# First layer of a two-layer kernel: one table instead of three, a running reference instead of the maximum, and the newest score clamped

## What is computed

```python
def step(buf, q_i):
    ki = jnp.concatenate([buf, jnp.zeros((B, 1, D), feature.dtype)], axis=1)
    scores = jnp.einsum('bwd,d->bw', q_i[:, None, :] * ki, w2_w) + w2_b[0]
    alpha = jax.nn.softmax(scores, axis=1)
    v_i = jnp.einsum('bwd,bw->bd', ki, alpha)
    new_buf = jnp.concatenate([buf[:, 1:, :], v_i[:, None, :]], axis=1)
    return (new_buf, v_i)
```

## Time and profile before

| | us |
|---|---|
| median of 3 runs | 3037.22 (3034.18 to 3037.38) |
| the profiled execution: its time | 3035.86 |
| the profiled execution: its span, first to last instruction | 3034.1 |
| busy in the span: VectorE | 2372.2 |
| busy in the span: TensorE (matmul) | 1531.9 |
| busy in the span: ScalarE | 1369.9 |
| busy in the span: GpSimd | 170.9 |

### The profile page before, as it was taken

How to read it: one execution, slowest core, us unless ns; L and a number is a source line. 1 busy time by engine, 2 the same in 40 slices (tenths; PEclk the granted TensorE clock), 3 DMA queues, 4 the chain that set the end, 5 groups by cost and what they waited for, 6 DMA issues and landing times.

```text
span 3034.1 us, 43821 instructions
## 1 busy us (share of the span) xinstructions
PE 1531.9 (50%) x8061; PEld 738.3 (24%) x8061; DVE 2372.2 (78%) x15872; ACT 1369.9 (45%) x3634; POOL 170.9 (6%) x259
## 2 busy tenths in 40 slices
PE   3001011011010010010159999999899988999796
PEld 1000000000000000000012224544245533445354
DVE  5999999999999999999678886777567765777523
ACT  1333333333333333333606666566665666556532
POOL 3000000000000000000101100100001000110000
PEclk9999999999999999999969999999999999999899
DMA  4000000000000000000340210020201101020100
GB/s 108 1 1 1 1 1 1 1 1 1 1 1 1 1 1 1 1 1 1 71 91 1 71 36 1 1 64 8 44 1 36 36 12 33 1 64 8 25 1 8
DMA packets 59766, 56.10 MB, mean 18 GB/s; under 512 B 6602, under 2 KB 43124, under 8 KB 59488
## 3 DMA queue, kind: packets, MB, share of 16 engines
q1 hardware_dynamic: 59488, 53.20, 7.4%
HBM read 29.98 MB, written 22.54 MB: 17 GB/s over the span
## 4 chain that ended last, share of the span: by engine, by line
PE 40%; ACT 3%; DVE 3%; issue 3%; DMA 1%; SPq 0%; ACTq 0%; DVEq 0%
PE p_o L1178 8%; PE bank L1232 8%; PE s L1213 7%; PE bank L1239 7%; PE s L1203 7%; ACT pt L951 2%; DVE nm_half L1026 2%; PE bank L1259 1%; ACT L951 1%; PE bank L1228 1%; PE bank L1251 0%; ACT hid L956 0%; PE bank L1275 0%; PE bank L1286 0%; DVE xa L1003 0%
## 5 line engine op out<-in xcount | busy, mean ns | idle before, releaser
L1026 DVE TENSOR_REDUCE nm_half<-s 128x1 f32<-128x512 f32 x1088 | 700.6, 685 | 250.0 <-PE s L1203 241.5
L951 ACT ACTIVATE pt<-s 128x512 f32<-128x512 f32 x1024 | 567.0, 596 | 416.2 <-PE s L1213 415.6
L197 ACT ACTIVATE ex<-row,nmax 128x65 f32<-128x65 f32 x960 | 336.0, 350 | 925.1 <-DVE nmax L299 837.7
L257 DVE SCALAR_TENSOR_TENSOR junk<-ex,tab 128x65 f32<-128x65 f32 x2850 | 620.7, 219 | 1.4 <-issue 0.2
L360 PE MATMUL p_s<-tab,bdg 128*128 128x32 f32 x120 | 31.9, 406 | 829.6 <-DVE tab L262 829.6
L1213 PE MATMUL s<-qs,ks 128*128 128x512 bf16 x1024 | 390.6, 389 | 68.0 <-ACT pt L951 56.4
L1203 PE MATMUL s<-ks,qs 128*128 128x512 bf16 x1088 | 389.1, 389 | 23.5 <-DMA qs<-zeros 20.3
L262 DVE TENSOR_TENSOR tab<-raw,rz 128x1 f32<-128x1 f32 (+1 forms) x1890 | 285.4, 151 | 3.2 <-issue 1.1
L1178 PE MATMUL p_o<-pt,va 128*9 128x512 f32 x2048 | 274.2, 608 | 0.1
L1239 PEld LDWEIGHTS bank<-w_W,hid 128*128 128x128 f32 x2048 | 257.8, 192 | 44.2 <-ACT hid L956 13.9
L291 DVE SCALAR_TENSOR_TENSOR junk<-ex,rz,row 128x65 f32<-128x65 f32 x930 | 265.3, 285 | 3.0 <-issue 2.7
(11 more groups left out here) (178 smaller groups left out, 1527.1 us busy)
## 6 DMA issues: line engine op xcount, KB each, us to landing
parts_dram<-parts SPq DMA_DIRECT2D x60, 256.0 KB, 3.6
qs<-parts_dram SPq DMA_DIRECT2D x38, 192.0 KB
ks<-parts_dram SPq DMA_DIRECT2D x38, 192.0 KB
h_dram<-f SPq DMA_DIRECT2D x20, 128.0 KB, 2.5
hq<-h_dram SPq DMA_DIRECT2D x5, 512.0 KB, 5.1
x<-in_x SPq DMA_DIRECT2D x4, 512.0 KB, 8.9
w_W<-in_W SPq DMA_DIRECT2D x1, 2048.0 KB
w_W<-in_W SPq DMA_DIRECT2D x8, 256.0 KB
```

The lines of the kernel that those rows point to most:

```text
L197: nc.scalar.activation(ex[:, r % 2, :], row[:, r % 2, 1:], ACT.Exp, bias=nmax[:, r % 2:r % 2 + 1], accum_out=z[:, r % 2:r % 2 + 1]).then_i ...
L257: nc.vector.scalar_tensor_tensor(junk[:, g, :], ex[:, k, :], 1.0, tab[:, g, r:r + ROW], ALU.mult, ALU.mult, accum_out=raw[:, g:g + 1]).the ...
L951: nc.scalar.activation(pt[:, i % 4, tokens(t)], s2[t][:, :], ACT.Exp, scale=SCALE).then_inc(s_exp, 1)
L1026: nc.vector.reduce_max(nm_half[:, t, head // 2 % 2, head % 2, q:q + 1], s1[k % 3][:, :], AX.X, negate=True).then_inc(s_max, 1)
```

## The change

The score plane and one coefficient plane become one table per chunk (`tab[:, c % 2, :]`, with a column more in front). A row holds negated scores until its step has been broadcast; then GpSimd multiplies its window by zero (`other` is 0 on the row's own partition, 1 elsewhere), and from its own step on the row collects coefficients: the column sum adds `rz` on the row's own partition (`at_own`). So one sum per step writes both the scores of later rows and the coefficients of earlier ones. That sum is a `tensor_tensor_reduce` with two pointer scalars, (ex * table) * rz summed from at_own on.

The maximum per row goes. In its place each row has a reference, the running minimum of the negated scores less 40 (`SPAN`), kept in the column ahead of the window, updated by VectorE (`least`) and broadcast along with the row; the exponential takes it as its bias. The newest score is clamped against it in the instruction that normalises it.

The 32 columns are coefficients over the 32 steps' "old parts" y (an exponential of the row's old scores, `e_old`, times the old vectors), so that a chunk needs: `masked`, `low_old`, `e_old`, its transpose (step 5), two block products on GpSimd (steps 6 and 7), y and its transpose on TensorE, a factor per row and `kf` at the end, one product for the scores of the next chunk instead of two, and one for the new vectors. Half of the next chunk's table is written at step 24. The pacing increments (`s_pace`) go.

VectorE, per chunk:

```diff
             for c in range(NC):
+                t = tab[:, c % 2, :]
                 dve.wait_ge(s_scores, c + 1)
...
+                nc.vector.stream_shuffle(row[:, 0, 3:3 + WIN], t[:, 1:1 + WIN], [0] * L).then_inc(s_first, 1)
+                nc.vector.stream_shuffle(row[:, 1, 2:2 + WIN], t[:, 1:1 + WIN], [1] * L).then_inc(s_first, 1)
+                dve.wait_ge(s_first, 2 * c + 1)
+                nc.vector.tensor_reduce(low[:, 0:1], row[:, 0, 3:3 + WIN], AX.X, ALU.min).then_inc(s_low, 1)
+                dve.wait_ge(s_first, 2 * c + 2)
+                nc.vector.tensor_reduce(low[:, 1:2], row[:, 1, 3:2 + WIN], AX.X, ALU.min).then_inc(s_low, 1)
+                dve.wait_ge(s_low, 2 * c + 1)
+                reference(c, 0, low[:, 0:1]).then_inc(s_ref0, 1)
+                dve.wait_ge(s_low, 2 * c + 2)
+                reference(c, 1, low[:, 1:2]).then_inc(s_ref0, 1)
+                dve.wait_ge(s_ref0, 2 * c + 2)
+                nc.vector.tensor_copy(ref[:, c % 2, 0:2], row[:, 0:2, 1]).then_inc(s_ref2, 1)
+
+                dve.wait_ge(s_masked, c + 1)
+                nc.vector.tensor_reduce(low_old[:, :], masked[:, :], AX.X, ALU.min).then_inc(s_low_old, 1)
+                dve.wait_ge(s_low_old, c + 1)
+                nc.vector.tensor_scalar(t[:, 0:1], low_old[:, :], 0.0, -SPAN, ALU.min, ALU.add).then_inc(s_base, 1)
```

VectorE, per step (what stands before is in the listing, L281 to L310):

```diff
+                    if last:
+
+                        dve.wait_ge(s_refs, (L - 2) * (c + 1))
+                        dve.wait_ge(s_ref2, c + 1)
+                        nc.vector.scalar_tensor_tensor(junk[:, 0, 0:L], ref[:, c % 2, :], 1.0, own[:, :], ALU.mult,
+                                                       ALU.mult, accum_out=ref_own[:, :]).then_inc(s_ref_own, 1)
                     dve.wait_ge(s_exp, n + 1)
                     nc.vector.reciprocal(rz[:, k:k + 1], z[:, k:k + 1]).then_inc(s_rz, 1)
                     if not last:
+                        if r:
+                            dve.wait_ge(s_row, (L - 2) * c + r)
+                        nc.vector.scalar_tensor_tensor(junk[:, 0, :], ex[:, k, 0:WIN], 1.0, row[:, 1 - k, 2:2 + WIN],
+                                                       ALU.mult, ALU.mult, accum_out=raw[:, k:k + 1]).then_inc(s_new, 1)
+
+                    dve.wait_ge(s_rz, n + 1)
+                    nc.vector.tensor_tensor(at_own[:, k:k + 1], own[:, r:r + 1], rz[:, k:k + 1], ALU.mult)\
+                        .then_inc(s_own_rz, 1)
                     if not last:
                         dve.wait_ge(s_new, (L - 1) * c + r + 1)
+                        if not r:
+                            dve.wait_ge(s_ref0, 2 * c + 2)
+                        nc.vector.tensor_scalar(row[:, 1 - k, 2 + WIN:3 + WIN], raw[:, k:k + 1], rz[:, k:k + 1],
+                                                row[:, 1 - k, 1:2], ALU.mult, ALU.max).then_inc(s_newest, 1)
+
+                    dve.wait_ge(s_own_rz, n + 1)
+                    dve.wait_ge(s_zeroed, (L - 1) * c + min(r, L - 2) + 1)
+                    if last:
+                        dve.wait_ge(s_col, n)
+                    nc.vector.tensor_tensor_reduce(junk[:, 1, :], ex[:, k, 0:WIN], t[:, 1 + r:1 + r + WIN],
+                                                   rz[:, k:k + 1], at_own[:, k:k + 1], ALU.mult, ALU.add,
+                                                   accum_out=t[:, 1 + WIN + r:2 + WIN + r]).then_inc(s_col, 1)
+                    dve.wait_ge(s_col, n + 1)
                     if r < L - 2:
+                        if r:
+                            dve.wait_ge(s_least, (L - 2) * c + r)
+                        else:
+                            dve.wait_ge(s_base, c + 1 + min(c, NC - 2))
+
+                        nc.vector.tensor_scalar(t[:, r + 1:r + 2], t[:, r + 1 + WIN:r + 2 + WIN], -SPAN, t[:, r:r + 1],
+                                                ALU.add, ALU.min).then_inc(s_least, 1)
+                        dve.wait_ge(s_least, (L - 2) * c + r + 1)
+                        nc.vector.stream_shuffle(row[:, k, 1:2 + WIN], t[:, r + 1:r + 2 + WIN], [r + 2] * L)\
                             .then_inc(s_row, 1)
+                    if r == 5:
+                        dve.wait_ge(s_eold, c + 1)
+                        nc.vector.transpose(e_old_t[:, :], e_old[:, :]).then_inc(s_eold_t, 1)
+                    if r == 24 and c + 1 < NC:
+                        dve.wait_ge(s_old, c + 1)
+                        relative(tab[:, 1 - c % 2, 1:1 + L], slice(0, L)).then_inc(s_table, 1)
+                dve.wait_ge(s_factor, c + 1)
+                nc.vector.tensor_scalar(kf[:, :], t[:, 1 + WIN:], factor[:, :], None, ALU.mult).then_inc(s_kf, 1)
```

GpSimd, per chunk (before: three copies and two block products):

```diff
             for c in range(NC):
+                t = tab[:, c % 2, :]
+                pool.wait_ge(s_table, 2 * c + 1)
+                nc.gpsimd.tensor_tensor(masked[:, :], t[:, 1:1 + WIN], tri[:, :], ALU.add).then_inc(s_masked, 1)
+
+                pool.wait_ge(s_first, 2 * c + 2)
+                nc.gpsimd.tensor_scalar(t[:, 1:1 + WIN], t[:, 1:1 + WIN], other01[:, :], None, ALU.mult)\
+                    .then_inc(s_zeroed, 1)
+                if c:
+                    pool.wait_ge(s_kf, c)
+                    blocks(bdk[:, :], kf[:, :]).then_inc(s_bdk, 1)
+                for r in range(L - 2):
+                    k = r % 2
+                    pool.wait_ge(s_row, (L - 2) * c + r + 1)
+
+                    nc.gpsimd.tensor_scalar(t[:, r + 2:r + 2 + WIN], t[:, r + 2:r + 2 + WIN], other[:, r + 2:r + 3],
+                                            None, ALU.mult).then_inc(s_zeroed, 1)
+                    nc.gpsimd.tensor_copy(ref[:, c % 2, r + 2:r + 3], row[:, k, 1:2]).then_inc(s_refs, 1)
+                    if r == 6:
+                        pool.wait_ge(s_eold_t, c + 1)
+                    if r in (6, 7):
+                        blocks(bde[:, r - 6, :], e_old_t[:, L * (r - 6):L * (r - 5)]).then_inc(s_bde, 1)
+                    if r == 20 and c + 1 < NC:
+                        nc.gpsimd.memset(tab[:, 1 - c % 2, 1 + WIN:], 0.0).then_inc(s_base, 1)
```

```diff
+                    nc.scalar.activation(ex[:, k, :], row[:, k, 3:], ACT.Exp, bias=row[:, k, 1:2], scale=-1.0,
+                                         accum_out=z[:, k:k + 1]).then_inc(s_exp, 1)
```

More of the change, by code:

```diff
@@ L55, in window_attention @@
         mask = sb("mask", [P, B, L])
+        later = sb("later", [P, B, L])
+        tri = sb("tri", [P, WIN])
+        own, other, other01 = sb("own", [P, L]), sb("other", [P, L]), sb("other01", [P, 1])
         wq = sb("wq", [P, D])
         bq = sb("bq", [P, 1])
[L58 to L61, removed]
+        w2, w2_neg = sb("w2", [P, 1]), sb("w2_neg", [P, 1])
+        b0, b0_neg = sb("b0", [P, 1]), sb("b0_neg", [P, 1])
         stats = sb("stats", [P, NK, 6])
@@ L81, in window_attention @@
         rz = sb("rz", [P, 2])
-        junk = sb("junk", [P, 4, ROW])
-        raw = sb("raw", [P, 3])
+        at_own = sb("at_own", [P, 2])
+        raw = sb("raw", [P, 2])
+        junk = sb("junk", [P, 2, WIN])
+        masked = sb("masked", [P, WIN])
+        low_old = sb("low_old", [P, 1])
+        e_old, e_old_t = sb("e_old", [P, WIN]), sb("e_old_t", [P, WIN])
+        bde = sb("bde", [P, 2, P])
+        yh, yt = sb("yh", [P, D]), sb("yt", [P, P])
+        bdg, bdk = sb("bdg", [P, P]), sb("bdk", [P, P])
+        ref_own, factor = sb("ref_own", [P, 1]), sb("factor", [P, 1])
+        kf = sb("kf", [P, L])
         pf = ps("pf", [P, 2, 4 * P])
@@ L166, in _ @@
[L166 to L172, removed]
-                pool.wait_ge(s_pv, c + 1)
-                for g in range(2):
-                    last = nc.gpsimd.tensor_tensor(
-                        bdc[:, g, :].rearrange("p (b j) -> p b j", b=B),
-                        tab[:, 1 + g, WIN:].unsqueeze(1).broadcast_to((P, B, L)), mask[:, :, :], ALU.mult)
@@ L180, in _ @@
+            pool.wait_ge(s_kf, NC)
+            blocks(bdk[:, :], kf[:, :]).then_inc(s_bdk, 1)
         @block.scalar
@@ L364, in _ @@
-            for g in range(2):
-                ins = nc.tensor.matmul(p_v[:, 0:D], bdc[:, g, :], v_all[:, NC + g, :], start=g == 0, stop=g == 1)
-            ins.then_inc(s_pv, 1)
+                    ins = nc.tensor.matmul(p_s[q, L * g:L * g + L], qt[:, k, q], vt[:, q], start=True, stop=True)
+                return ins
+            pe.wait_ge(s_qt, 8)
+            pe.wait_ge(s_vt0, 2)
+            against(2, vt1, 0)
+            against(2, vt2, 1).then_inc(s_scores, 1)
+            pe.wait_ge(s_vall, 2)
@@ L371, in middle @@
+            pe.wait_ge(s_yh, NC)
+            pe.wait_ge(s_bdk, NC)
+            nc.tensor.matmul(p_v[:, 0:D], bdk[:, :], yh[:, :], start=True, stop=True).then_inc(s_pv, 1)
 def middle(nc, io, xt, x1_dram, h_dram):
```

242 lines of the change are left out of this document (112 added, 130 removed).

## The result

The changed kernel takes 3252.76 us (median of 4 runs, 3251.04 to 3254.80), the kernel before 3037.30 (4 runs) beside it: ratio 1.0711, interval 1.0693 to 1.0730. The forecast was 3117, range 2975 to 3205. The kernel got slower, as forecast, but by 215 us instead of 80, outside the range.

The account below looks back on a forecast made before the run. The prediction took each step's chain of dependent operations (sum, new score, maximum, exponential) as the bound. Steps of 1.44 instead of 1.36 us, 900 times, gave 72, chunks 8: +80 on 3037.2, so 3117 us, range 2975 to 3205.

Parts of the forecast that it names:

- the hold term: Each step: own, the one-element product, is held until POOL's zeroing ends, delaying newest 0.06 us; step 1.44 instead of 1.38.
- rival 4: Whole step: only the count of VectorE instructions matters, 0.28 us less per step, 2785 us; chance 0.04.
- rival 2: Column sum to least: the column sum is cheap, 0.25 instead of 0.38, step 1.29, 2974 us; chance 0.20.
- the wait for POOL: Each step: POOL's zeroing takes 0.25 us, ending at 0.57, so the column sum at 0.71 doesn't wait.
- the set-up: Ahead of the first step: lost waits and gained constants count as nothing, plus or minus 2 us.
- rival 1: Each step: own isn't held by POOL, nor block products holding; step 1.38, +18, 3055 us; chance 0.18.
- Rival 3: Each step: the score sum itself is held by POOL to 0.57, step 1.55, 3216 us; chance 0.12.
- With the chunks: Odd steps of each of the 30 chunks: changes sum to +0.27 us a chunk, 8 us in all.
- r = 7 and 8: Steps beside POOL's block products, placed at r = 6 and 7: column sum held, +0.3 us a chunk, bounds 0 and 0.6.
- r = 5 and r = 24: Transpose and half table between shuffle and score sum: about 0.1 and 0.2 us, +0.3 a chunk.
- Step 30: Step of each chunk without a shuffle: next reciprocal after 1.11 us instead of 1.36, -0.25.
- The boundary: Between chunks, table to table: +0.36, -0.46 and +0.07 us, together about 0.

Follow-up runs that it names:

- e7: Changed kernel with zeroing on ScalarE, memsets behind VectorE's first two key copies, and one reference per chunk instead of a running one: 2837.68 us, ratio 0.9344.
- e9: As e4, but GpSimd's scratch operation is a plain 64-element copy instead of the product with a pointer; one execution: 3083.96 us.
- e2: Changed kernel with GpSimd's zeroing written as a product of two tensors instead of a tensor and a pointer scalar: 3108.57 us, ratio 1.0245.
- e3: Changed kernel with the zeroing on ScalarE behind the exponential; GpSimd keeps only its copy of the reference: 3077.74 us, ratio 1.0134.
- e8: As e4, but GpSimd's scratch product has an immediate factor in place of the pointer; one execution: 3088.93 us.
- e4: As e3, but GpSimd still does its pointer product each step, on a scratch buffer nobody waits for: 3074.54 us, ratio 1.0130.
- e1: Changed kernel with GpSimd's memsets of the second layer's stacks moved back behind the first query block: 3249.19 us, ratio 1.0703.
- e10: Kernel before the change, with GpSimd's first memset ahead of its copy of the queries; one execution: 3038.74 us against 3039.28.

## Why the prediction was right or wrong

**Right: the method and most of its chain.** Dependences followed once round gave 1.38 without a hold. Without the wait the step would be 1.35 by step 0's spacing. By its terms: score sum 0.26 against 0.26 measured; newest 0.51 against 0.53; newest to column sum 0.20 against 0.18 (step 0); column sum to least 0.38 against 0.39; least to shuffle 0.29 with the hold term left out against 0.25. So fewer instructions on VectorE bought nothing: rival 4's count of instructions falls, as rows 3 had said, and rival 2 (a cheap column sum, step 1.29) falls with 0.39. The Trainium skill (VectorE: DVE Perf Modes, Rules for kernel authors) advises to minimise the count; e7 shows which instruction's removal pays, one in the chain (0.25 us for 0.21 of work). The count itself, "13 instructions to 10", was misread: a step has 14 rows on VectorE before and 10 after with the shuffle's mask load, 13 and 9 without it.

**That the sign came out right is mostly luck.** Of the +80, 72 came from a step of 1.44, three quarters of it from a hold of own that did not happen in the change. Unheld, the forecast had 1.38; with the measured spacings and no wait the step would have been 1.35, about no change in the loop. The two things that made the kernel slower, the wait for POOL and the set-up, were both priced at nothing.

**Wrong, first: "I take 0.25 in all, to 0.57. The column sum at 0.71 doesn't wait for it."** POOL's zeroing takes 0.48, its end is at +0.80, and the column sum starts another 0.15 after that. I priced the pointer on GpSimd between 0 and VectorE's 0.06, on top of a length scaled down from a copy; even the upper bound I kept, 0.35, was short. A copy of the same 64 elements measured 0.29 (e9), so scaling 0.29 for 128 elements to 0.24 was 0.05 off, and the pointer form is 0.19 above the copy, three times its dearest price in the text. The size was off, and the structure followed: a link that I had called covered became the bound. The plain step's +0.23 is this one term: 0.24 for the wait, on an unheld step of 1.35. No row of before showed a GpSimd operation with a pointer scalar in this size, and there the bound should have reached to a small operation twice as long, with the wait that it brings as a rival of its own: from a length of 0.39 on (0.32 + length > 0.71), and with the 0.15 from POOL's end to the column sum, which the forecast left out altogether, from 0.24 on. I had named this case among what would show the forecast wrong, but gave it no chance.

**Wrong, second: "Set-up loses the wait for qt and the b0 row, gains constants ... I count both as nothing, plus or minus 2 us."** It is +21.4. I had the hold between the two engines in hand, and did not ask what else the removed wait kept apart. The Trainium skill (SBUF — State Buffer, section SBUF: two separate sides) says that a VectorE operation in a fast two-port mode and a GpSimd one exclude each other for the whole instruction. The trace agrees: fp32 operations from SBUF to SBUF went from 336 to 1744 ns beside memsets, and one copy lasted 13.85.

**Wrong, third: "Here own ... is held to 0.57".** In the change own lasts 0.15 and newest comes unheld; rival 1 was right about own, but not by L262's row: that operation ended 0.05 behind POOL's copy, where a held one would have ended too, so the row couldn't tell. The hold appeared as soon as the zeroing read two tensors (e2: own 0.24, to 0.015 behind the zeroing's end), and beside a plain copy (e9: 0.18, to 0.013 behind the copy's end). Holding by a copy was read rightly from the rows; that a product with a pointer holds as a copy does was assumed. By that page own, with two inputs from SBUF, is held by any GpSimd operation that reads SBUF; the 0.15 beside the pointer product disagrees. Rival 3 (score sum held) falls too: it starts 0.06 ahead of POOL and took 0.22.

**With the chunks**, +0.27 forecast, -0.08 measured by the medians, beside the plain steps' 0.23. Right: the step beside POOL's copies (-0.08), and r = 7 and 8 beside the block products, 1.717 each, +0.25 together (0.3 forecast). Wrong: r = 5 and r = 24 take 0.16 and 0.22 longer, but the next step gives 0.11 and 0.17 of that back; 0.10 in all where I had 0.3. There the column sum still starts 0.15 behind the zeroing, and all that is lost is that the zeroing itself takes 0.53 instead of 0.48, twice. With that wait nearly gone (e3) the two cost 0.02 and 0.10: a late reciprocal alone costs little, since the score sum follows it after 0.04 instead of 0.13. Step 0 was not in the list and is 0.31 shorter than a plain one: 0.24 because it has no zeroing to wait for, and the most of the rest because no shuffle stands ahead of its score sum, which follows the reciprocal after 0.07 instead of 0.13. Step 30, "next reciprocal 1.11 instead of 1.36: -0.25", is 1.32, so -0.04: the next reciprocal stands in VectorE's order behind the step's column sum, which waits for the zeroing too. With the zeroing on ScalarE it is 1.18 (e3). The boundary, "about 0", is +0.07.

**The sum**, measured: 900 x 0.232 = 209, the chunks' own steps 30 x -0.08 = -2, boundaries +2, fewer late steps -10: the loop's 199. Set-up +21, the end -2: 218.

## What to carry to other kernels

When work moves to another engine inside a tight loop, price that engine's instruction in its exact form (pointer, immediate, two tensors, copy) and size, and add the way through the semaphore; if no row shows the form, let its bound reach to where it becomes the limit and give that case a chance. Fewer instructions on an engine that only looked full bought nothing here: look for the operations in the chain, here one of a single element at 0.25 us a step. A wait that is removed may have kept two engines from blocking each other; list what now starts earlier, down to the initialising memsets.

## What the runs showed of the hardware

- The late steps: before, they come in some chunks at every eighth step (chunk 8, counted from 0: steps 4, 12, 20, 28, each +0.29), after, about one in each chunk. What causes them wasn't tried; with them the change gains 10 us that no term of the forecast had.
- GpSimd, 128x64 fp32, beside VectorE's work: copy 0.29, two-tensor product 0.33, immediate product 0.40, pointer product 0.48 us. The form with less to read is the slower one. Whether the pointer form is as long with VectorE idle no run shows; once per chunk, ahead of the first step, it takes 0.44 (L188).
- The semaphore way: the column sum starts 0.14 to 0.15 after the end of POOL's or ScalarE's zeroing, in the change, e2 and e3 alike.
- Holding between VectorE and GpSimd shows in where the held operation ends. A one-element product of two tensors ends 0.01 to 0.02 behind a GpSimd copy (e9) or two-tensor product (e2, e7). Beside an immediate product it ends 0.12 ahead of that product's end (e8); beside a pointer product 0.24 ahead, with its usual 0.15 (the change, e4), or 0.12 ahead, with 0.18, at the steps in which it starts later (0.23 behind POOL instead of 0.09).
- The column sum, held by a block product, ended 0.08 behind it wherever it had started: 0.05 before that product (e8), or 0.06 (the change), 0.09 (e9) or 0.17 (e7) after its start. The sum beside a copy in the earlier trace rows ended in the same place, 615.33 against 615.26. Started 0.27 after (e3), it took its usual 0.34, ended 0.16 behind the product anyway and lost nothing: r = 7 and 8 take 1.40 there. In these runs a hold puts the end off to a fixed place; it isn't a sum added to the length.
- Starting first doesn't decide near ties: the column sum that had started 0.05 earlier was still held (e8), and so was a copy that started 0.012 before a memset (e1), but not one that started 0.016 before (e10).
- The first reciprocal of kernels whose set-up code is alike (e9's has two small memsets more) came at 76.0 (e2), 76.8 (e9), 80.1 (e3) and 81.2 (the change). Why it spreads wasn't tried; with the memsets behind the copies it was 59.1 to 59.6 in three kernels.
